# Causal triangles cleared by GpSimd after the exponential, and row sums taken over lots of four and two rounds

## The reference

```python
qkv = jnp.einsum('bsd,de->bse', x, W_qkv)
attn = jnp.einsum('bhqd,bhkd->bhqk', q, k) / math.sqrt(HEAD_DIM)
attn = attn + alibi_bias(seq_len, N_HEADS)[None] + causal_mask(seq_len)[None, None]
attn = jax.nn.softmax(attn, axis=-1)
y = jnp.einsum('bhqk,bhkd->bhqd', attn, v)
...
x = x + _L0_attn_ref(xn, W_qkv, W_o) + _L0_ffn_ref(xn, wg, W, b)
```

## Time and profile before

| what | us |
|---|---|
| time, median of 3 runs | 1774.7 (1774.01 to 1775.14) |
| the profiled execution's own time | 1770.8 |
| its span, first to last instruction | 1769.0 |
| span of one middle group of the attention (829.68 to 964.80) | 135.12 |
| in it PE / PEld / DVE / ACT / POOL busy | 134.71 / 69.06 / 96.34 / 76.36 / 65.13 |
| attention's first score product to its last value product | 390.42 to 1497.1 |

### The profile page before, as it was taken

How to read it: one execution, slowest core, us unless ns; L and a number is a source line. 1 busy time by engine, 2 the same in 40 slices (tenths; PEclk the granted TensorE clock), 3 DMA queues, 4 the chain that set the end, 5 groups by cost and what they waited for, 6 DMA issues and landing times. The chain is left out here.

```text
span 1769.0 us, 27986 instructions
## 1 busy us (share of the span) xinstructions
PE 1666.7 (94%) x9970; PEld 1011.5 (57%) x9971; DVE 1045.4 (59%) x2452; ACT 761.1 (43%) x1575; POOL 675.0 (38%) x643
## 2 busy tenths in 40 slices
PE   5999999679999999999999999999999998799898
PEld 4777777444545545554555554554554533688686
DVE  5433332467777766776766776776776700634366
ACT  2222222114554654655655555555555564411110
POOL 4500000004862553553554454454355365223350
PEclk9999999859999999999999999999999999899999
DMA  6655564571803703702801801900900500545596
GB/s 228 215 180 184 178 205 147 161 127 39 157 8 71 124 8 65 137 8 53 148 8 41 160 8 30 171 8 20 182 8 8 202 7 13 173 143 164 189 395 229
DMA packets 96927, 203.59 MB, mean 115 GB/s; under 512 B 10908, under 2 KB 28348, under 8 KB 91164
## 3 DMA queue, kind: packets, MB, share of 16 engines
q1 hardware_dynamic: 82984, 170.17, 36.9%
q0 software_dynamic: 9216, 23.47, 4.2%
q10 hardware_dynamic: 4608, 8.39, 1.6%
HBM read 122.46 MB, written 79.01 MB: 114 GB/s over the span
## 5 line engine op out<-in xcount | busy, mean ns | idle before, releaser
L1037 ACT ACTIVATE probs_sb<-score_ps 128x512 f32<-128x512 f32 (+3 forms) x1280 | 595.1, 546 | 486.5 <-PE score_ps L1106 223.7
L916 POOL TENSOR_TENSOR pair_sum<-probs_sb 128x512 f32<-128x512 f32 x384 | 480.7, 1284 | 422.0 <-ACT probs_sb L1037 333.4
L939 DVE TENSOR_REDUCE part_max<-max_ps 128x1 f32<-128x512 f32 x768 | 476.0, 679 | 248.3 <-PE max_ps L1071 248.0
L1071 PE MATMUL max_ps<-k_aug,q_aug 104*128 104x512 f32 (+3 forms) x1280 | 531.4, 427 | 27.2 <-DMA q_aug<-q_rows_d 19.8
L1103 PE MATMUL score_ps<-q_aug,k_aug 106*128 106x512 f32 (+3 forms) x1280 | 475.2, 392 | 13.0 <-DMA q_aug<-max_lo 8.9
L1071 PEld LDWEIGHTS max_ps<-k_aug,q_aug 104*128 104x128 f32 x1280 | 250.7, 197 | 183.7 <-issue 80.4
L1103 PEld LDWEIGHTS score_ps<-q_aug,k_aug 106*128 106x128 f32 x1280 | 243.7, 191 | 114.4 <-ACT probs_sb L1037 86.4
L1148 PE MATMUL acc_ps<-probs_sb,v_sb 128*32 128x512 f32 (+3 forms) x2560 | 291.1, 534 | 0.0
L935 DVE CUSTOM_DVE_ANT_0 max_ps<-max_ps,mask_row 128x384 f32<-128x384 f32 (+3 forms) x512 | 238.8, 514 | 48.7 <-PE max_ps L1071 45.5
L1148 PEld LDWEIGHTS acc_ps<-probs_sb,v_sb 128*32 128x32 f32 x2560 | 73.0, 110 | 118.1 <-issue 91.3
L623 DVE SCALAR_TENSOR_TENSOR st_lo<-group_ps,st_hi 128x512 fp32r<-128x512 f32 x64 | 44.3, 692 | 139.9 <-ACT st_hi L670 139.9
(11 more groups left out here) (175 smaller groups left out, 1737.9 us busy)
## 6 DMA issues: line engine op xcount, KB each, us to landing
k_aug<-k_hi_d SPq DMA_DIRECT2D x14, 1024.0 KB
q_aug<-q_hi_d SPq DMA_DIRECT2D x14, 1024.0 KB
slot_y_d<-y_rows SPq DMA_DIRECT2D x39, 256.0 KB, 2.0
xn_d<-xn SPq DMA_DIRECT2D x8, 1024.0 KB, 5.4
q_hi_d<-st_hi SPq DMA_DIRECT2D x32, 256.0 KB, 3.4
q_lo_d<-st_lo SPq DMA_DIRECT2D x32, 256.0 KB, 3.9
k_hi_d<-st_hi SPq DMA_DIRECT2D x32, 256.0 KB, 2.5
k_lo_d<-st_lo SPq DMA_DIRECT2D x32, 256.0 KB, 2.8
```

Source lines behind the costliest of these rows:

```text
L916: nc.gpsimd.tensor_tensor(pair_sum[:, p % 2, hh], probs[:, s0, hh], probs[:, s1, hh], ALU.add).then_inc(pair_added, 1)
L939: nc.vector.tensor_reduce(part_max[:, hh * QT + i, kc:kc + 1], max_ps[:, bank, 0:w], AX.X, ALU.max).then_inc(max_taken, 1)
L1037: nc.scalar.activation(probs[:, r % P_SLOTS, hh, off:CH], score_ps[:, (r * HG + hh) % S_BANKS, off:CH], ACT.Exp).then_inc(exp_done, 1)
L1071: nc.tensor.matmul(max_ps[:, bank, 0:w], q_aug[0:ROW_MAX, half, hh, i * P:(i + 1) * P], k_aug[0:ROW_MAX, half, hh, kc * CH:kc * CH + w], s ...
```

## The change

Three things are changed.

1. The mask. The bf16 mask products are gone. The queries and keys get 16 more rows (`steps_d`, rows 106 to 121), which subtract a large number from every 32-wide step that lies wholly in the masked part; diagonal score products read 122 rows instead of 106. What is left of the triangle is set to zero after the exponential by GpSimd (`clear`, one instruction over the four heads' 128x128 squares), and PE waits for it (`cleared`) in place of the exponential before the products of a diagonal round.
2. The row sums. Rounds off the diagonal go in lots: `LOT_SIZES` gives 4 rounds for chunk 1; 4, 2, 2 for chunk 2; 4, 2, 2, 2, 2 for chunk 3, so 9 products with ones for a group in place of 12. POOL makes 3 additions for each head in a lot of 4, the second and third into `quad_sum` in place.
3. The beginning. The maxima rows of chunk 0 of the first group are issued by ACT instead of SP. The 16 step rows are loaded once for each half of `q_aug` and `k_aug`: 2 transfers behind the first chunk's loads and 6 behind the last chunk's for group 0, 8 with the load of group 1. In group 0 the token transfers on POOL (`place_tokens`) go two at a time behind the additions and clears.

```diff
-PAIR_LAST = {p: r for r, p in PAIR_OF.items()}
+LOT_SIZES = {1: (4,), 2: (4, 2, 2), 3: (4, 2, 2, 2, 2)}
+QUAD_ROUNDS = []
...
+                def add_quad(t, first, exps, used, adds):
+
+                    r0, r1, *others = QUAD_ROUNDS[t]
+                    if not (first and t < 2):
+
+                        pool.wait_ge(quad_used, used + (t - 1))
+                    for hh in range(HG):
+                        pool.wait_ge(exp_done, exps + (r1 * HG + hh + 1))
+                        nc.gpsimd.tensor_tensor(quad_sum[:, t % 2, hh], probs[:, r0 % P_SLOTS, hh], probs[:, r1 % P_SLOTS, hh],
+                                                ALU.add).then_inc(added, 1)
+                    for r in others:
+                        for hh in range(HG):
+                            pool.wait_ge(exp_done, exps + (r * HG + hh + 1))
+
+                            pool.wait_ge(added, adds + (added_by(r) - 2 * HG + hh + 1))
+                            nc.gpsimd.tensor_tensor(quad_sum[:, t % 2, hh], quad_sum[:, t % 2, hh],
+                                                    probs[:, r % P_SLOTS, hh], ALU.add).then_inc(added, 1)
+
+                def clear(r, exps):
+
+                    cc, jb = ROUNDS[r]
+                    off = (jb - TPC * cc) * P
+                    square = probs[:, r % P_SLOTS, :, off:off + P]
+                    pool.wait_ge(exp_done, exps + (r + 1) * HG)
+                    nc.gpsimd.affine_select(out=square, in_=square, compare_op=ALU.is_ge, fill=0.0, base=0,
+                                            pattern=[[0, HG], [1, P]], channel_multiplier=-1).then_inc(cleared, 1)
...
-                            if e in PAIR_OF:
-                                act.wait_ge(pair_added, adds + ((PAIR_OF[e] + 1 - back * NPAIR) * HG))
+                            if e in QUAD_OF:
+                                act.wait_ge(added, adds + (added_by(e) - back * ADDS))
...
+                act.wait_ge(max_lo_done, 1)
+                for row, part in ((ROW_MAX, max_hi), (ROW_MAX + 1, max_lo)):
+                    for hh in range(HG):
+                        act.dma_start(q_aug[row:row + 1, 0, hh, 0:CH].bitcast(F32),
+                                      part[hh * TPC:(hh + 1) * TPC, 0].bitcast(F32)).then_inc(max_rows_loaded[0], 16)
...
-                    if diag:
-                        last = nc.tensor.matmul(score_ps[:, u % S_BANKS, off:off + P], m.ident_bf[:], m.mask_kq[:],
-                                                start=False, stop=True)
-                    last.then_inc(scored, 1)
...
+                    rows = slice(0, DIAG_ROWS if r in DIAG_OF else ROWS)
+                    nc.tensor.matmul(score_ps[:, u % S_BANKS, off:CH], k_aug[rows, half, hh, jb * P:(jb + 1) * P],
+                                     q_aug[rows, half, hh, cc * CH + off:(cc + 1) * CH], start=True, stop=True).then_inc(scored, 1)
...
-                    pe.wait_ge(exp_done, exps + (r + 1) * HG)
+                    if r in DIAG_OF:
+                        pe.wait_ge(cleared, g * NDIAG + DIAG_OF[r] + 1)
+                    else:
+                        pe.wait_ge(exp_done, exps + (r + 1) * HG)
```

More of the change, by code:

```diff
@@ L62, with added_by @@
 NPAIR = len(PAIR_OF) // 2
-PAIR_LAST = {p: r for r, p in PAIR_OF.items()}
+LOT_SIZES = {1: (4,), 2: (4, 2, 2), 3: (4, 2, 2, 2, 2)}
+QUAD_ROUNDS = []
+for _c, _sizes in LOT_SIZES.items():
+    _off = [r for r, (c, jb) in enumerate(ROUNDS) if c == _c and jb < TPC * _c]
+    for _n in _sizes:
+        QUAD_ROUNDS.append(_off[:_n])
+        _off = _off[_n:]
+NQUAD = len(QUAD_ROUNDS)
+QUAD_OF = {r: t for t, rounds in enumerate(QUAD_ROUNDS) for r in rounds}
+QUAD_LAST = [rounds[-1] for rounds in QUAD_ROUNDS]
+ADDS_OF = [(len(rounds) - 1) * HG for rounds in QUAD_ROUNDS]
+ADDS = sum(ADDS_OF)
+def added_by(r):
+    t = QUAD_OF[r]
+    return sum(ADDS_OF[:t]) + HG * max(1, QUAD_ROUNDS[t].index(r))
+DIAG_OF = {r: n for n, r in enumerate(r for r in range(NR) if r not in QUAD_OF)}
+NDIAG = len(DIAG_OF)
+FIRST_SUM = [min(r for r, (cc, _) in enumerate(ROUNDS) if cc == c and (r not in QUAD_OF or r - 2 in QUAD_LAST))
+             for c in range(QC)]
 LAST_ROUND = [max(r for r, (cc, _) in enumerate(ROUNDS) if cc == c) for c in range(QC)]
@@ L162 @@
              for c in range(QC) for k in range(INVERT_STEPS)}
[L164 to L165 removed]
+SUMMED_OR_CLEARED = sorted([*QUAD_LAST, *DIAG_OF])
+Y_BEFORE_ROUND = {min(r for r in SUMMED_OR_CLEARED if r > (LAST_ROUND[c] + 2 + INVERT_STEPS) % NR):
+                  ((LAST_ROUND[c] + 2 + INVERT_STEPS) // NR, c) for c in range(QC)}
 class Memory:
@@ L289, in project_and_route @@
         key_rel = sb("key_rel", [P, KEYS], F32)
+        steps = sb("steps", [STEPS, 2, CH], F32)
         lg = sb("lg", [P, NT, E], F32)
@@ L819, in load_qk, with load_steps @@
                     sp.dma_start(q_aug[ROW_ALIBI:ROWS, half, :, here].bitcast(F32), m.q_rows_d[:, :, here]).then_inc(loaded, 16)
+                    if g == 1:
+                        load_steps(half, here, loaded)
+                def load_steps(half, here, loaded):
+                    for aug, t in ((q_aug, 0), (k_aug, 1)):
+                        for c in range(here.start, here.stop, CH):
+                            sp.dma_start(aug[ROWS:DIAG_ROWS, half, :, c:c + CH].bitcast(F32),
+                                         m.steps_d[t].unsqueeze(1).to_broadcast([STEPS, HG, CH])).then_inc(loaded, 16)
                 def load(g, half):
@@ L900, in step @@
-                    for p in range(NPAIR + 1):
-                        if p in Y_BEFORE_PAIR:
-                            back, cc = Y_BEFORE_PAIR[p]
+                    exps, used, adds = base(pool, g, NSU), base(pool, g, NQUAD), base(pool, g, ADDS)
+                    for r in SUMMED_OR_CLEARED:
+                        if r in Y_BEFORE_ROUND:
+                            back, cc = Y_BEFORE_ROUND[r]
                             if not (first and back):
                                 normalise(g - back, cc)
-                        if p == NPAIR:
-                            break
-                        if first and 1 <= p <= NT // SCATTERS:
-                            place_tokens(p - 1)
-                        r1 = PAIR_LAST[p]
-                        s0, s1 = (r1 - 1) % P_SLOTS, r1 % P_SLOTS
-                        if not (first and p < 2):
-                            pool.wait_ge(pair_used, used + (p - 1))
-                        for hh in range(HG):
-                            pool.wait_ge(exp_done, exps + (r1 * HG + hh + 1))
-                            nc.gpsimd.tensor_tensor(pair_sum[:, p % 2, hh], probs[:, s0, hh], probs[:, s1, hh],
-                                                    ALU.add).then_inc(pair_added, 1)
@@ L919, in _ @@
+                        if r in DIAG_OF:
+                            clear(r, exps)
+                        else:
+                            add_quad(QUAD_OF[r], first, exps, used, adds)
+                        if first and r in pieces:
+                            place_tokens(pieces[r])
                 groups(pool, step)
@@ L1102, in score_unit, with quad_product @@
                         pe.wait_ge(exp_done, exps + (e + 1 - back * NSU))
[L1103 to L1110 removed]
+                    rows = slice(0, DIAG_ROWS if r in DIAG_OF else ROWS)
+                    nc.tensor.matmul(score_ps[:, u % S_BANKS, off:CH], k_aug[rows, half, hh, jb * P:(jb + 1) * P],
+                                     q_aug[rows, half, hh, cc * CH + off:(cc + 1) * CH], start=True, stop=True).then_inc(scored, 1)
+                def quad_product(t, start, adds):
                     for hh in range(HG):
[L1113 to L1114 removed]
+                        pe.wait_ge(added, adds + (added_by(QUAD_LAST[t]) - HG + hh + 1))
+                        last = nc.tensor.matmul(den_ps[hh * DH:(hh + 1) * DH, :], m.ones[:], quad_sum[:, t % 2, hh],
                                                 start=start, stop=False)
[L1116 removed]
+                    last.then_inc(quad_used, 1)
                 def probs_of(g, r, exps):
@@ L1168, in step @@
                                 pe.wait_ge(max_rows_loaded[cc % 2], MAX_ROWS * (g * (QC // 2) + cc // 2 + 1))
+                            if first and hh == 0 and ROUNDS[r] == (1, TPC):
+                                pe.wait_ge(steps_loaded, STEP_ROWS * (QC - 1))
                             score_unit(half, r, hh, first, exps)
```

86 lines of the change are left out of this document (49 added, 37 removed).

## The result

The changed kernel takes 1755.5 us (median of 4 runs, 1754.4 to 1761.8) against 1774.9 before in the same comparison: a ratio of 0.9902, 95% interval 0.9885 to 0.9918. That is 19.4 us less where 37.2 were forecast (1738). The profiled execution's span is 1752.7 us against 1769.0, 16.3 less.

What follows compares the result with a forecast made beforehand. PE was taken to hold the product phases, but to be tied to DVE and ACT in score phases. Terms -20.6 - 12.6 + 3 - 7 = -37.2 us gave 1737.5, said as 1738; range 1702 to 1766.

Steps and rivals of the forecast that it cites:

- the rival in which POOL takes the place: Slower additions on POOL cost 8 to 16 us in all, giving 1746 to 1754; heavier form (1752 to 1771) 0.13.
- Row sums, -20.6: Product phases: 24 fewer products with ones in 8 groups, 0.86 us each, since PE holds the pace there.
- Masks, -12.6: Diagonal score phases without mask products: 1.65 us a group, 11.6 in seven, and 1.0 in the last group.
- The second halves of the diagonals: Visits 5, 11, 19: DVE runs unbroken, so about 0 gained; shortening as much as first halves would disprove the forecast.
- The beginning, -7.0: Maxima rows issued by ACT: first score near 383.4, after 1.3 us for two transfers and 0.5 us more.
- POOL, +3: POOL's added work: 1.5 us given back in the last group, 0.25 in each of six middle groups at round 20.
- "The six later step transfers ... cost nothing": Group 0's six later step transfers, 0.8 MB, needed a chunk later and lying in the queue's idle time: no cost.

Runs made afterwards that it cites:

- early_pairs: The changed kernel with the second-half step rows issued early, behind chunk 1's maxima rows, and all lots of four replaced by lots of two: 1764.0 us.
- split_pe_masks: `load_split` with the masks undone (bf16 mask matmuls on PE, no clears, no step rows): 1759.2 us.
- steps_not_waited: The changed kernel with step transfers left in place but counted in their own semaphore, awaited at group 1's first score: 1745.0 us, ratio 0.9834.
- steps_ahead: The changed kernel with the eight step transfers issued at the head of group 1's load instead of its end: 1755.6 us.
- steps_early: The changed kernel with the second half's eight step transfers issued behind group 0's chunk 1 maxima rows, not behind group 1's load: 1751.5 us, ratio 0.9874.
- load_split: `steps_not_waited` with group 0's six later step transfers and group 1's first two transfers behind chunk 1's maxima rows, group 1's steps behind `v_sb`: 1739.0 us.
- the fills: Two or five of visit 1's maxima products run twice in groups 1 to 7, added to the kernel with four last-group fill matmuls: 1730.7 and 1727.8 us.
- the fill: Four overwritten 512-column matmuls put into a PE wait in the last group, on the kernel with chunk 2's normalising moved later: 1734.9 us, last group 122.82.

## Why the prediction was wrong

Its sign was right and its size was not: 16.3 us of span instead of 37.2. That 1755.5 still lies inside the stated 1702 to 1766 is luck: that part was given to the rival in which POOL takes the place, and POOL isn't what held the kernel up. Step by step:

- **Row sums, -20.6.** Right as a unit: 0.86 for each, 2.6 in a middle group. Undone alone, with no load in the way, they are worth 13 to 17, because the last group gains nothing.
- **Masks, -12.6.** Right: 1.65 forecast for a group, 1.8 (`early_pairs` against before) and 1.9 (`split_pe_masks`) measured; 2.1 in the last group instead of 1.0. The second halves of the diagonals stayed as they were (0.00, 0.00 and 0.06 us shorter), so PE doesn't hold those.
- **The beginning, -7.0.** -7.1, for the reason given; two misses cancel. The two step transfers cost 2.0 us and not 1.3, and the 0.5 us allowed between the maxima and the first score wasn't needed.
- **POOL, +3.** No idle time of PE ends at a clear (its weight load waits some 0.25 us for one, at visit 5 of each group from group 1 on, and the phase is as long as before), and none shows the 0.25 us in middle groups. ACT waits for POOL at round 20 in the last group alone, not in the middle ones. In the last group ACT is late by POOL (3.69 us ahead of round 32) and PE by 1.64, forecast 1.5. What the step lacks is what follows the wait, below.
- **"The six later step transfers ... cost nothing", and no word of eight more.** This step failed. The sum counted the two transfers ahead of the first product and group 0's six, and left out the eight that group 1's load issues, though the section on the change names them and the kernel counts them in the semaphore that PE waits for. With the load's own lateness they cost 17.84 us. Group 0's six were not free for certain either: where chunk 1's maxima rows stand behind them PE waited 0 us (after), 2.2 (`steps_not_waited`), 3.3 (`steps_ahead`), 5.1 (`steps_early`) and 6.4 (`early_pairs`).
- **A floor that was not priced.** Making visits shorter moves the date at which the next group's load is wanted, not the date at which it lands. Group 1 misses it by 5.6 us, of which the clock's part is 1.9, and three middle groups by 0.65, 0.55 and 1.18.
- **The clock.** The forecast has no term for it. In the changed kernel it falls in two middle groups, whose chunk 0 takes 18.85 and 18.56 us instead of 16.94, and twice in the last group, 1.57 us in the product phase behind visit 7 and 1.28 in that behind visit 16. With the wait of 1.64 that is why the last group gained nothing.

The missing 20.9 us add up: +17.8 for the wait in group 0, +2.5 in the last group (-2.1 forecast, +0.4 measured), +2.8 in the middle ones (-23.9 and -21.1), and -2.0 because group 0 apart from its wait gained 6.2 instead of 4.2, in part by the clock; some -0.2 are the beginning and what lies outside the attention.

That the wait for the step rows is the larger part of the miss is shown by `steps_not_waited`, which moves no transfer and takes 12.2 of the 17.84 us away; `load_split`, which moves the steps and two of group 1's ordinary transfers as well, takes the rest. That want of work in visit 1 lets the clock fall in the middle groups is shown by the fills and borne out by the two kernels with mask products, one execution of each. In the last group the fill keeps the clock, but mask products didn't: `split_pe_masks` has both falls there. What decides between two groups alike to 0.02 us, of which one has the fall, is open.

## What to carry to other kernels

Go through every call site of a new transfer in the diff, and for each ask which semaphore it counts in and who waits for that, with the rest of the queue ahead of it. When PE gets less to do, list what it will then want earlier: the next load's landing is a date that doesn't move with it. And look at the granted clock of every stretch after an edit that removes matmuls; where it falls, a few matmuls for nothing in a wait can be worth more than they cost.

## What was not expected of the hardware

The transfers of the step rows, into 16 partitions, kept the DMA engines as busy as the load's into 32, at a half to two thirds of the rate (91 and 133 GB/s, with `v_sb` beside them, against 203). The granted clock fell to 0.50 (1.2 of 2.4 GHz) in some groups and not in others with the same instructions at the same offsets; two more 512-column matmuls in visit 1 kept it at 1.00 in all six, and even five took no time that can be seen.
